# A gated recurrence on one core: bias operand padded to 128 rows, two time blocks in one loop body, filler products regrouped

## What is computed

```python
def _L0_cond_ref(x, ada_emb, base_layer, w1, b1, w2, b2, ln_g, ln_b):
    ae = _layernorm(ada_emb, ln_g, ln_b)
    h = jax.nn.gelu(ae @ w1 + b1, approximate=False)
    xw = h @ w2 + b2
    x_a, x_b = jnp.split(xw, 2, axis=-1)          # each to (b, 256, 8)
    layer = base_layer[None, :, :] + jnp.einsum('bdr,bkr->bdk', x_a, x_b)
    return x + jnp.einsum('btc,bco->bto', x, layer)

x = x + _L0_cond_ref(x, cond, ...)                 # y
xW = jnp.einsum('ntd,dh->nth', x, Wx) + b
next_h = jnp.tanh(prev_h @ Wh + xw)                # 1024 times, from h0 = cond
out = x + h
```

## Time and profile before

| | us |
|---|---|
| median of 3 runs (816.26 to 816.67) | 816.48 |
| the profiled execution | 815.04 |
| its span, first to last instruction | 813.2 |
| PE busy | 756.9 (93%) |
| PEld busy | 696.4 (86%) |
| ACT busy | 397.6 (49%) |
| DVE busy | 258.7 (32%) |

### The profile page before, as it was taken

How to read it: one execution, slowest core, us unless ns; L and a number is a source line. 1 busy time by engine, 2 the same in 40 slices (tenths; PEclk the granted TensorE clock), 3 DMA queues, 4 the chain that set the end, 5 groups by cost and what they waited for, 6 DMA issues and landing times.

```text
span 813.2 us, 48323 instructions
## 1 busy us (share of the span) xinstructions
PE 756.9 (93%) x21105; PEld 696.4 (86%) x21105; DVE 258.7 (32%) x1411; ACT 397.6 (49%) x3092; POOL 6.2 (1%) x17
## 2 busy tenths in 40 slices
PE   5799999999999999999999999999999999999997
PEld 4688888888888888888888888888888888888885
DVE  6433323333333323332323332323332323332322
ACT  6344444444444444444444444444444444444444
POOL 3000000000000000000000000000000000000000
DMA  7000000000000000000000000000000000000000
GB/s 263 6 10 6 6 6 5 3 6 5 6 6 5 3 6 5 6 6 5 3 6 5 6 6 5 3 6 5 6 6 5 3 6 5 6 6 5 3 6 6
DMA packets 12100, 9.76 MB, mean 12 GB/s; under 512 B 1813, under 2 KB 11056, under 8 KB 12080
## 3 DMA queue, kind: packets, MB, share of 16 engines
q1 hardware_dynamic: 11984, 9.45, 4.0%
q0 software_dynamic: 96, 0.02, 0.0%
HBM read 7.36 MB, written 2.10 MB: 12 GB/s over the span
## 4 chain that ended last, share of the span: by engine, by line
PE 88%; ACT 5%; issue 3%; DMA 1%; SPq 1%; DVE 1%; DVEq 0%; another core or an unknown queue 0%
PE acc L312 45%; PE pre L312 15%; PE acc L295 9%; PE p_y L276 7%; ACT h_pre L452 5%; PE pre L295 5%; PE acc L292 2%; PE p_xo L271 2%; DMA x_in<-x_dram 1%; PE pre L292 1%; PE p_xo L266 1%; SPq L212 1%; PE p_y L409 0%; SPq L209 0%; DVE lay_s L675 0%
## 5 line engine op out<-in xcount | busy, mean ns | idle before, releaser
L312 PE MATMUL acc<-h_pre,wh_s 128*128 128x2 f16 x8192 | 496.5, 167 | 37.6 <-issue 6.9
L312 PEld LDWEIGHTS acc<-h_pre,wh_s 128*128 128x128 f16 x8192 | 378.8, 106 | 85.6 <-ACT h_pre L452 70.4
L452 ACT ACTIVATE h_pre<-pre 128x4 f16<-128x4 f32 x1023 | 177.6, 174 | 398.6 <-PE pre L312 398.6
L556 DVE TENSOR_TENSOR h_lo<-h_f,h_pre 128x4 f16<-128x4 f32 x1024 | 167.5, 164 | 535.3 <-ACT h_f L458 534.2
L312 PE MATMUL pre<-h_rnd,wh_s 128*128 128x2 f16 x4092 | 259.0, 167 | 0.0
L312 PE MATMUL acc<-h_lo,wh_s 128*128 128x2 f16 x4096 | 253.2, 166 | 0.0
L312 PEld LDWEIGHTS acc<-h_lo,wh_s 128*128 128x128 f16 x4096 | 189.2, 105 | 0.0
L312 PEld LDWEIGHTS pre<-h_rnd,wh_s 128*128 128x128 f16 x4092 | 187.5, 106 | 0.0
L458 ACT ACTIVATE h_f<-acc 128x4 f32<-128x4 f32 x1024 | 177.9, 174 | 0.6 <-PE acc L312 0.6
L460 ACT ACTIVATE h_rnd<-acc 128x4 f16<-128x4 f32 x1022 | 171.8, 168 | 0.0
L295 PE MATMUL acc<-y_s,wx_s 128*128 128x16 f16 x2048 | 113.6, 177 | 0.0
(11 more groups left out here) (76 smaller groups left out, 161.9 us busy)
## 6 DMA issues: line engine op xcount, KB each, us to landing
w_f<-w_dram SPq DMA_DIRECT2D x8, 512.0 KB, 9.4
x_in<-x_dram SPq DMA_DIRECT2D x32, 64.0 KB, 2.3
out_dram<-o_row SPq DMA_DIRECT2D x64, 32.0 KB, 1.9
w_f<-w_dram SPq DMA_DIRECT2D x1, 256.0 KB, 2.8
base_f<-base_dram SPq DMA_DIRECT2D x1, 256.0 KB, 11.2
wh_f<-wh_dram SPq DMA_DIRECT2D x1, 256.0 KB, 10.7
wx_f<-wx_dram SPq DMA_DIRECT2D x1, 256.0 KB, 10.6
cond_r<-cond_dram SPq DMA_DIRECT2D x1, 2.0 KB
```

Source lines behind the costliest of these rows:

```text
L312: return nc.tensor.matmul(dst[:, mo, :], wh_s[:, pw, ki, mo * P:(mo + 1) * P], h[:, par, ki, :], start=False, stop=True, skip_group_check= ...
L452: nc.scalar.activation(h_pre[:, n % 2].rearrange("p m b -> p (m b)"), src, func, scale=scale).then_inc(s_hpre[(n // HALF) % 2], 1)
L556: nc.vector.tensor_sub(h_lo[:, par].rearrange("p m b -> p (m b)"), h_f[:, slot, :], h_pre[:, par].rearrange("p m b -> p (m b)")).then_inc( ...
```

## The change

Three edits are made together.

1. `b_w` and `ones` have 128 rows instead of 3. `ones` is all ones, `b_w` is set to zero by an added memset on POOL before the three parts of the bias are put in rows 0 to 2; `s_ones` counts to 2 now, and POOL waits for it ahead of the transfer into `b_w`.
2. The loop bodies of PE and DVE hold two blocks, [B, A, B, A], run 15 times instead of 30. ACT's loop, which ran 31 times [B, A], runs 15 times [B, A, B, A], with one more [B, A] behind it.
3. No filler product stands after step 15 of a half. The first 8 layer products go after steps 13 and 14 of A (before: 12 after 13 to 15), the other 24 after steps 0 and 2 to 5 of B (before: 20 after 0 and 2 to 4), and the 54 input products in B go 9 at a time after steps 9 to 14 (before: 8 at a time after steps 9 to 15). `s_ymm`, for which DVE waits to finish y, is signalled after step 5 instead of step 4.

```diff
-        b_w = sb("b_w", [3, D], F16)
-        ones = sb("ones", [3, HALF * NB], F16)
+        b_w = sb("b_w", [P, D], F16)
+        ones = sb("ones", [P, HALF * NB], F16)
...
+            nc.gpsimd.memset(b_w[:, :], 0.0).then_inc(s_ones, 1)
...
-            pool.dma_start(b_w[:, :], b_parts[0:1, :, :]).then_inc(s_bw, 16)
+            pool.wait_ge(s_ones, 2)
+            pool.dma_start(b_w[0:3, :], b_parts[0:1, :, :]).then_inc(s_bw, 16)
...
-            EARLY, LATE = LAYER[:12], LAYER[12:]
+            EARLY, LATE = LAYER[:8], LAYER[8:]
...
-                    if u >= 13:
+                    if 13 <= u < HALF - 1:
                         layer_products(share(EARLY, 4, u - 13))
...
-                    if 2 <= u < 5:
+                    if 2 <= u < 6:
                         product = layer_products(share(LATE, 5, u - 1))
-                    if u == 4:
+                    if u == 5:
                         product.then_inc(s_ymm, 1)
...
-                    if u >= 9:
-                        input_products(A, share(INPUT, 8, u - 9))
+                    if 9 <= u < HALF - 1:
+                        input_products(A, share(INPUT, 9, u - 9))
...
-            with pe.Fori(0, NBLOCK - 2):
-                half_b()
-                half_a()
+            with pe.Fori(0, (NBLOCK - 2) // 2):
+                for _ in range(2):
+                    half_b()
+                    half_a()
...
-            with act.Fori(0, NBLOCK - 1):
-                half_block(B)
-                half_block(A)
+            with act.Fori(0, (NBLOCK - 2) // 2):
+                for _ in range(2):
+                    half_block(B)
+                    half_block(A)
+            half_block(B)
+            half_block(A)
```

More of the change, by code:

```diff
@@ L436, in _ @@
             pe.wait_ge(s_bw, 16)
-            pe.wait_ge(s_ones, 1)
+            pe.wait_ge(s_ones, 2)
             input_products(A, INPUT[:BEFORE])
             half_a(first=True)
-            with pe.Fori(0, NBLOCK - 2):
-                half_b()
-                half_a()
+            with pe.Fori(0, (NBLOCK - 2) // 2):
+                for _ in range(2):
+                    half_b()
+                    half_a()
             half_b()
@@ L682, in _ @@
             half_a(first=True)
-            with dve.Fori(0, NBLOCK - 2):
-                half_b()
-                half_a()
+            with dve.Fori(0, (NBLOCK - 2) // 2):
+                for _ in range(2):
+                    half_b()
+                    half_a()
             half_b()
```

## The result

The changed kernel takes 860.7 us in the median of 4 runs (856.7 to 862.3), the kernel before 816.4 us in the runs beside it: a ratio of 1.0535, 95% interval 1.0499 to 1.0571. The direction is as forecast and the time lies just inside the range, but the change is 44 us where 19 were forecast.

A forecast was written before the change was run, and what follows sets the result against it. The PE, ACT, PE round trip of 0.73 us per step was taken as the bound. 815.0 - 19.4 - 5.0 = 790.6; + 43.4 = 834.0; with the median 1.4 us above the profiled execution, 835.4 us, range 806 to 862.

The forecast's parts named there:

- What bounds the kernel: Chain of time steps: round trip PE, ACT, PE sets 0.73 us; six bias steps lose 0.61 us per block, the branch 0.33.
- (1): Bias products padded to their neighbours' row count: both load delays at each bias pair go, -19.4 us.
- Rival C: Bias products: the delay is from operand or bank, not the 3 rows, so padding gives nothing, 854.8 us; chance 0.06.
- (2): Regrouped filler products in PE's gaps, later `s_ymm` and clears at a half's end: no change in time.
- (3): PE's loop branch: 14 taken instead of 29, fifteen at 0.33 us go, -5.0 us.
- (4): PE's body of 169 KB isn't kept: one fetch wait of 3.1 us at each of 14 branches, +43.4 us.
- rival A: PE's loop: all 169 KB are kept, no instruction packets appear inside the loop, 792.0 us, 3% faster; chance 0.12.
- 83 KB: PE's code in one pass of the old loop, 5.2 pieces of 16 KB, kept and executed again without a fetch.
- 3.1 us: Fetch wait at each branch back: a transfer's fixed 2.1 us plus 1.0 us for the packet.
- 792.0: Whole kernel: forecast time in us without the fetches, with the padding and fewer branches counted.
- rival D: Branch back: more than one wait, second piece late too, or a clock falling; over 5.0 us each, above 862; chance 0.03.

The follow-up runs named there:

- straight code: Changed kernel with PE's 30 blocks written out without a loop, ACT and DVE keeping their loops of two blocks: 786.6 us, ratio to before 0.964.
- the kernel with one-block bodies: Changed kernel with loops of one block on all three engines, padding and new fillers kept: 796.8 us, ratio to before 0.977.
- the runs with 1,515 and 1,707 instructions: Padding, new fillers and one-block bodies, with 3 or 6 small products added behind each step in PE's loop: 809.0 and 1016.6 us.
- 5 misses: Changed kernel with five blocks in PE's loop body and 6 passes, so five branches back: 813.2 us, ratio to before 0.998.

## Why the prediction was right or wrong

**Right:** *What bounds the kernel*, the pace of 0.73 us with six bias steps and the branch over it: the bias steps fell to the pace with the padding, the step over the branch in straight code. *(1)* -19.4 us for the padding: padding alone measured 796.6 against 815.1, 18.5 us. Rival C fell, and with it the reading by which a small row count is free: the loads last as long, but going to 3 rows and back costs 0.21 us, and at 128 rows it is gone. Why a change of the row count costs time is open. *(2)* nothing for the fillers: right beside the padding, 1.3 us of loss without it. *(3)* 0.33 us for a branch that hits: the steps over it are 0.31 us over the pace in the kernel with one-block bodies, and straight code is 10.2 us under that kernel, for its 29 branches back, 0.35 each with the entry and exit. *(4)* that PE doesn't keep 169 KB; rival A fell at the point named for it, with 190 packets where there were 16. The Trainium skill, "Runtime: NRT & Kernel Launch", section on instruction fetch, gives 128 KiB for PE, in blocks of 16 KiB: eight pieces of 16 KB are what the runs with 1,515 and 1,707 instructions show, with one of them taken by the piece ahead, so a body of 109 KB is not kept. (The prediction's 83 KB counts 1,024 B to the KB and its 169 KB 1,000; its 5.2 and 10.3 pieces are both right.)

**Wrong:** the price in *(4)*. Its "3.1 us" holds one wait at each branch, since "the following pieces come ahead of use, as in the straight part"; that step failed, as the second piece came 1.48 us late. The terms:

| at each of 14 branches | forecast | measured |
|---|---|---|
| first fetch, over the 0.33 of a branch that hits | 3.1 us | 3.68 - 0.33 = 3.35 us |
| second piece late | none | 1.48 us |
| sum times 14 | 43.4 us | 67.6 us |

792.0 + 67.6 = 859.6 us, against 860.7 measured. The first term was 0.25 us short, and that it came so near is in part luck: the 2.1 us of a data transfer, from issue to landing, hold its own packets already, and the 1.1 us of the packet were added on top. The trace has 1.0 us ahead of the packet and 1.5 us between its end and PE's first load, which the sum had nowhere. The second term was left out, and it is 20.7 of the 24.2 us by which the sum over the branches was short. It was the mechanism of rival D, which had a chance of 0.03 and a price of over 5.0 us; the two waits cost 4.83. That the time lies inside the range is luck as well: its upper end, 5.0 us, was meant for one slow fetch, not for two.

The trace of the kernel before held what was needed to price it, nearly. In its first pass the last instruction packet starts at 64.63 us, and 190 instructions follow up to the branch, of the body's 1,323; so a piece begins some 1,133 instructions behind the target, and, 256 at a time, one some 110 behind it. It lies at 92, since a packet starts somewhat behind the border that asks for it. A fetch of 3.1 us against 1.6 us of work leaves 1.5 us. The error was to take the straight part's rule, where PE has a whole piece to run through while the next is fetched, over to a branch that lands near the end of a piece.

## What to carry to other kernels

Count an engine's instructions in a loop body before making it larger: here PE kept a body that touches 7 pieces of 256 instructions and not one that touches 8, and the miss turns a branch of 0.2 us into one of 3.4 to 3.9 us, with a second stall behind it unless the target stands near the start of a piece. Against straight code, 29 hits cost 10 us, 14 misses 74 and 5 misses 27: at 5.3 us each, two misses already cost what 29 hits do. And a matmul with few rows amid ones with 128 can cost more than its own time; filling it up to the rows of its neighbours with zeros took 2.3% off this kernel.

## What the runs showed that was not expected

- A fetch after a branch takes 3.6 us from the branch to the first load (3.4 to 3.9), though its packet takes 1.1 us: 1.0 us passes ahead of the packet and 1.5 us behind it.
- The place of the code counts: 80 instructions ahead of the loop gave 882.4 us, none 860.7 and 100 gave 840.3.
- Once a body exceeds what is kept by a piece, all its pieces are fetched in each pass (9 packets a pass with 1,707 instructions), not only the one that has no room.
